# Merging the preparation into attention 0, and moving the split of the maxima ahead of the weight sums

## The reference

```python
mod = (_silu(L0_c) @ L0_wmod).reshape(16, 6, 1, -1)      # sa, ca, ga, sb, cb, gb; ga, gb kept at 0.25 or more in size
h = _layernorm(x) * (1 + ca) + sa
x = x + ga * attn0(h)        # 16 heads of 8; k and v through a 32-wide latent
h = _layernorm(x) * (1 + cb) + sb
x = x + gb * ffn0(h)         # ternary weights: 128 -> 512 -> 512 -> 512 -> 128, silu gate, two exact gelus
# block 1: the same frame with a second mod (L1), a causal attention of 4 heads with a memory, and 8 experts, top 2
```

## Time and profile before

| | |
|---|---|
| timed, three executions | 852.59, 853.60, 857.45 us |
| profiled execution | 857.48 us, span 855.7 us |
| mean granted TensorE clock | 0.939 |
| busy over the span | PE 85%, DVE 73%, ACT 63%, POOL 45% |
| preparation | 0.7 to 20.2 us |
| attention 0 | 21.1 to 321.2 us |
| ffn0, attention 1, router, experts | 322.2 us to the end |

### The profile page before, as it was taken

The page is one execution under the profiler, slowest core; times in us unless marked ns, Lnnn a source line. Parts: engine busy times, 40 slices in busy tenths (PEclk is TensorE's granted clock), DMA queues, the critical chain, the costliest instruction groups (busy, mean ns, idle before and its releaser), DMA issues. The chain is left out here.

```text
span 855.7 us, 17153 instructions
## 1 busy us (share of the span) xinstructions
PE 729.7 (85%) x5738; PEld 507.8 (59%) x5738; DVE 624.4 (73%) x1423; ACT 540.4 (63%) x1195; POOL 388.9 (45%) x484
## 2 busy tenths in 40 slices
PE   3367999999998886789999998489998939999996
PEld 3222333333333325788989998367776728888774
DVE  3176898998988525787777764278889857888884
ACT  0215777777776544668888885388887715655653
POOL 3533554645442001042111000489998625776664
PEclk9999999999999855999999999699999968999998
DMA  5365545444552004000000000000000250644430
GB/s 144 52 88 75 90 74 78 70 73 73 72 76 35 3 1 140 1 1 1 1 2 1 1 2 1 2 3 1 2 2 1 76 130 25 172 124 120 129 97 25
DMA packets 81178, 44.19 MB, mean 52 GB/s; under 512 B 7121, under 2 KB 79298, under 8 KB 80962
## 3 DMA queue, kind: packets, MB, share of 16 engines
q1 hardware_dynamic: 81090, 43.07, 25.3%
HBM read 27.83 MB, written 2.25 MB: 35 GB/s over the span
## 5 line engine op out<-in xcount | busy, mean ns | idle before, releaser
L597 DVE TENSOR_REDUCE att_negmax<-att_p_max 128x2 f32<-128x512 f32 x256 | 169.9, 687 | 42.4 <-PE att_p_max L481 40.1
L686 ACT ACTIVATE att_probs<-att_p_sT 128x1024 f32<-128x1024 f32 x128 | 130.9, 1025 | 60.2 <-PE att_p_sT L487 57.4
L481 PE MATMUL att_p_max<-att0p_QK 48*128 48x256 bf16 x512 | 102.8, 292 | 25.4 <-DVE att_negmax L597 11.6
L2061 POOL TENSOR_TENSOR moe_z_lo<-moe_z,moe_z_hi 128x512 fp32r<-128x512 f32 x64 | 96.8, 1525 | 55.1 <-ACT moe_z_hi L2014 54.5
L487 PE MATMUL att_p_sT<-att0p_QK 51*128 51x256 bf16 x512 | 101.5, 291 | 0.0
L952 POOL TENSOR_TENSOR ffn0s_rstd<-ffn0s_var_eps,top_minus_half 128x2 f32<-128x2 f32 x16 | 11.2, 700 | 191.9 <-DVE ffn0s_var_eps L939 191.9
L481 PEld LDWEIGHTS att_p_max<-att0p_QK 48*128 48x128 bf16 x512 | 29.1, 96 | 105.8 <-DVE att_negmax L597 50.2
L509 PE MATMUL att_p_o<-att_probs,att0p_V 128*32 128x256 f32 x1024 | 88.1, 419 | 0.1
L906 PE MATMUL ffn0s_p_h<-ffn0s_u_hi,top_ffn_all 128*128 128x256 f32 x256 | 71.3, 311 | 16.7 <-DVE ffn0s_u_lo L1167 16.2
L1167 DVE TENSOR_TENSOR ffn0s_g_lo<-ffn0s_g,ffn0s_g_hi 128x512 fp32r<-128x512 f32 x64 | 49.1, 782 | 43.8 <-ACT ffn0s_g_hi L1111 42.5
L2052 DVE TENSOR_TENSOR moe_z<-moe_act_u,top_ffn_all 128x512 f32<-128x512 f32 x64 | 73.1, 1143 | 2.2
(11 more groups left out here) (250 smaller groups left out, 1952.1 us busy)
## 6 DMA issues: line engine op xcount, KB each, us to landing
top_ffn_all<-combine SPq DMA_DIRECT2D x32, 512.0 KB, 6.6
att0p_QK<-att_parts SPq DMA_DIRECT2D x192, 64.0 KB
top_X<-in_L_attn_x SPq DMA_DIRECT2D x4, 512.0 KB, 7.0
att_raw<-in_L_ffn_h_w SPq DMA_DIRECT2D x8, 256.0 KB, 3.7
out_x<-top_X SPq DMA_DIRECT2D x8, 256.0 KB, 2.3
top_wo_all<-gates SPq DMA_DIRECT2D x4, 256.0 KB
top_gbo_all<-gates SPq DMA_DIRECT2D x4, 256.0 KB
top_wo_all<-gates SPq DMA_DIRECT2D x1, 1024.0 KB, 6.1
```

The costliest lines, as they stand in the source:

```text
L481: mm = pe.matmul(bank(at)[:, i, :], QK[r][rows, g, 0, i * P:(i + 1) * P], QK[r][rows, g, 1, :], start=True, stop=True)
L597: dve.tensor_reduce(negmax[:, :, w, g], bank(at)[:], AX.X, ALU.max, negate=True).then_inc(drained, 1)
L686: act.activation(probs[g % 2][:, t % 2], p_sT[t % 2][:], ACT.Exp).then_inc(exped, 1)
L2061: pool.tensor_tensor(z_lo[e % RING][:], z[e % RING][:], z_hi[e % RING][:].bitcast(F32), ALU.subtract).then_inc(z_lo_ready, 1)
```

## The change

1. `prepare` as a block is gone. `preparation(k, a, sb, sem, banks)` makes the same tensors inside `attention0` and hands out functions that the engines' programs call between their steps; its PSUM banks are those of the transposed scores.
2. The host packs the small inputs. `start_cols` [128 x 292] holds c of both blocks transposed, four bias columns, Wq and Wo with heads already in order; `start_rows` [32 x 385] holds Wl transposed, Wk, Wv and bl. x comes as [128 x 4096], so that a partition's share of several batches is one run in DRAM. PE's transposes of c and Wl and DVE's permutations go.
3. x is loaded in the parts `X_PARTS = [(0, 1), (1, 4), (4, 10), (10, 16)]` (batches), the first two at the start, the other two behind the stacks of batches 0 and 1. Each part and each modulation weight has its own semaphore.
4. Before step 0 only sa and ca of block 0 are made (4 of the 24 modulation instructions); the rest, the output bias and the gates come after step 1. The rows of the gates are stored in SP's step 1, and their loads move to steps 2 to 5, POOL's use of them to steps 3 to 6.
5. At the end the four sums stand in step 18 in slots 2, 6, 7 and 8, behind the split (slots 0 and 1). A product of a column of 0/1 marks with itself on PE counts the inexact rows in place of the way through DRAM, and the flag is made in step 19, slot 8.

```diff
+    def sp_loads(sp):
+        sp.dma_start(k.cols[:], a["start_cols"]).then_inc(c.cols_loaded, 16)
+        sp_x(sp, 0)
+        sp.dma_start(wmod[:, 0, :], a["L0_wmod"]).then_inc(wmod_loaded[0], 16)
+        sp.dma_start(rows[:], a["start_rows"]).then_inc(rows_loaded, 16)
+        sp_x(sp, 1)
+        sp.dma_start(wmod[:, 1, :], a["L1_wmod"]).then_inc(wmod_loaded[1], 16)
...
+    def pe_first(pe):
+        pe.wait_ge(rows_loaded, 16)
+        pe.matmul(p_v[:, 0:D], wlT, wk, start=True, stop=True)
+        pe.matmul(p_v[:, D:2 * D], wlT, wv, start=True, stop=True).then_inc(w_made, 1)
+        pe.matmul(p_b[:, 0:1], wk, lat_bias, start=True, stop=True)
+        pe.matmul(p_b[:, 1:2], wv, lat_bias, start=True, stop=True).then_inc(bias_made, 1)
+        pe.wait_ge(c_silu, 1)
+        pe.wait_ge(wmod_loaded[0], 16)
+        for j in (SA, CA):
+            mm = pe_mod(pe, 0, j)
+        mm.then_inc(mod_first_made, 1)
+        pe.wait_ge(c.ident_ready, 2)
...
+    def pe_rest(pe):
+        pe.wait_ge(c.bias_ready, 1)
+        pe.matmul(p_bo[:, 0:1], k.wo0, bv_col[:], start=True, stop=True).then_inc(bo_made, 1)
+        pe.wait_ge(c.mod_first_ready, 1)
+        for j in (GA, SB, CB, GB):
+            pe_mod(pe, 0, j)
+        pe.wait_ge(wmod_loaded[1], 16)
+        for j in range(6):
+            mm = pe_mod(pe, 1, j)
+        mm.then_inc(mod_rest_made, 1)
...
+                if n == B + 2 and slot in (2, 6, 7, 8):
+                    dve_sum_lo(dve, (2, 6, 7, 8).index(slot))
+                if n == B + 2 and slot == 9:
+                    dve_lo_any(dve)
+                    dve_lo_bad(dve)
+                if (n, slot) == FLAG_AT:
+                    dve_flag(dve)
...
-            if n == 0:
-                sp.wait_ge(gate_rows_ready, 1)
-                sp.dma_start(k.gates_dram, gate_rows[:]).then_inc(gates_stored, 16)
...
+            if n in (1, 2):
+                c.sp_x(sp, n + 1)
             if n == 1:
+                sp.wait_ge(gate_rows_ready, 1)
+                sp.dma_start(k.gates_dram, gate_rows[:]).then_inc(gates_stored, 16)
+            if n == 2:
                 sp.wait_ge(gates_stored, 16)
...
+        def pe_flag(pe):
+            at = RING["flag", 0]
+            pe.wait_ge(lo_bad_ready, 1)
+            at_least(pe, drained, at - 1)
+            pe.matmul(bank(at)[0:1, 0, 0:1], lo_bad[:], lo_bad[:], start=True, stop=True).then_inc(filled, 1)
...
+            c.pool_constants(pool)
+            c.pool_zero_v(pool, 0)
             pool_normalise(pool, 0)
+            c.pool_zero_v(pool, 1)
             for n in range(B + 3):
                 pool_step(pool, n, n % NB)
+                if n == 0:
+                    c.pool_zero_v(pool, 2)
+                    c.pool_zero_v(pool, 3)
...
-            pe_turn_gates(pe)
+            c.pe_first(pe)
             for n in range(LAST):
                 pe_step(pe, n, n % NB)
+                if n == 1:
+                    c.pe_rest(pe)
+                    pe_turn_gates(pe)
...
+            c.dve_ones(dve, 0)
+            c.dve_silu(dve)
             dve_stats(dve, 0)
+            c.dve_weights(dve)
+            c.dve_mod_first(dve)
+            c.dve_v_ones(dve, 0)
             for n in range(LAST):
                 dve_step(dve, n)
+                if n == 0:
+                    c.dve_ones(dve, 1)
+                    c.dve_v_ones(dve, 1)
+                if n == 1:
+                    for r in (2, 3):
+                        c.dve_v_ones(dve, r)
+                    c.dve_mod_rest(dve)
+                    for r in (2, 3):
+                        c.dve_ones(dve, r)
                 if n == B:
                     dve_scales(dve)
-                if n in (B + 1, B + 2):
-                    for quarter in range(2):
-                        dve_sum_lo(dve, 2 * (n - B - 1) + quarter)
-                if n == B + 2:
-                    dve_lo_any(dve)
-            dve_flag(dve)
```

More of the change, by code:

```diff
@@ L70 @@
 LATE_LOADED = 16 * LATE_LOADS
-X_LOADS = 4
-X_LOADED = 16 * X_LOADS
+X_PARTS = [(0, 1), (1, 4), (4, 10), (10, 16)]
+COLS = 2 * B + 4 + 2 * D
 class Names:
@@ L369, in attention0 @@
         p_m16 = p_m[:].bitcast(BF16)
+        c = preparation(k, a, sb, sem, [p_sT[n][:, w].rearrange("p i q -> p (i q)") for n in range(2) for w in range(2)])
         gates_turned = sem("gates_turned")
@@ L433, in attention0 @@
                     RING["O", n - 4] = len(RING)
+                if (n, slot) == FLAG_AT:
+                    RING["flag", 0] = len(RING)
                 if batch_valid(n - 2):
@@ L452, in pe_q @@
             pe.wait_ge(hT_ready, b + 1)
-            pe.matmul(p_m[:, 0:S], k.wq0[:], hT[:], start=True, stop=True)
+            if b == 0:
+                pe.wait_ge(c.wkv_ready, 1)
+            pe.matmul(p_m[:, 0:S], k.wq0, hT[:], start=True, stop=True)
         def pe_k(pe, b):
@@ L566, in pe_step @@
                     pe_turn_O(pe, t)
+                if (n, slot) == FLAG_AT:
+                    pe_flag(pe)
                 if slot >= SCORES:
@@ L837, in dve_scales, with dve_lo_bad @@
             dve.tensor_scalar(k.w3_gate[:], k.mod[:, 0, GB, :], k.w3_scale[:, 0:1], None, ALU.mult)
-        def dve_flag(dve):
-            dve.wait_ge(lo_row_loaded, 32)
-            dve.tensor_reduce(lo_flag[:, 0:1], lo_row[:], AX.X, ALU.max).then_inc(flag_step, 1)
-            dve.wait_ge(flag_step, 1)
-            dve.tensor_scalar(lo_flag[:, 1:2], lo_flag[:, 0:1], 0.0, None, ALU.not_equal).then_inc(flag_step, 1)
-            dve.wait_ge(flag_step, 2)
-            dve.tensor_copy(k.rows_inexact[:], lo_flag[:, 1:2])
+        def dve_lo_bad(dve):
+            dve.wait_ge(lo_any_ready, 1)
+            dve.tensor_scalar(lo_bad[:], lo_any[:], 0.0, None, ALU.not_equal).then_inc(lo_bad_ready, 1)
+        def pe_flag(pe):
[3 more added lines that the diff above has]
+            pe.matmul(bank(at)[0:1, 0, 0:1], lo_bad[:], lo_bad[:], start=True, stop=True).then_inc(filled, 1)
+        def dve_flag(dve):
+            at = RING["flag", 0]
+            dve.wait_ge(filled, at + 1)
+            dve.tensor_scalar(lo_flag[:], bank(at)[0:1, 0, 0:1], 0.0, None, ALU.not_equal).then_inc(drained, 1)
+            dve.wait_ge(drained, at + 1)
+            dve.tensor_copy(k.rows_inexact[:], lo_flag[:])
         def pool_step(pool, n, r):
@@ L2118, in build @@
         k.mod = sb("mod", [P, 2, 6, B])
-        k.wq0, k.wk0, k.wv0, k.wo0 = (sb(f"w{x}0", [P, D]) for x in "qkvo")
+        k.cols = sb("cols", [P, COLS])
+        k.wq0, k.wo0 = (k.cols[:, 2 * B + 4 + n * D:2 * B + 4 + (n + 1) * D] for n in range(2))
+        k.wk0, k.wv0 = (sb(f"w{x}0", [P, D]) for x in "kv")
         k.bq0, k.bk0, k.bo0 = (sb(f"b{x}0", [P, 1]) for x in "qko")
@@ L2137, in build @@
         k.mask16 = sb("mask16", [P, P], BF16)
-        k.flag_dram = nc.dram_tensor("flag", (P, 1), F32, kind="Internal").ap()
         k.bg = sb("bg", [P, E])
@@ L2196 @@
     arrays, aps = {}, {}
[L2197 to L2204 removed]
+    for name, array in laid_out(inputs).items():
         arrays[f"in_{name}"] = array
```

347 lines of the change are left out of this document (159 added, 188 removed).

## The result

The changed kernel took 846.6 us (median of 14 executions, 840.3 to 853.4) where the kernel before took 857.4 in the same rounds (851.2 to 864.9): a ratio of 0.9876, 95% interval 0.9842 to 0.9911. The profiled execution of the changed kernel took 841.4 us (span 839.5), 16.0 less than that of before.

The account below looks back on a forecast made before the run. Bounds: a latency chain at the start, TensorE at 1.2 GHz at the end. 857.5 less 12.5 (front), 1.8 (end) and 6.4 (clock) gave 836.8, or 832.9 from the median; forecast 835 us, range 829 to 846.

Parts of the forecast that it names:

- every later step has time to spare for its 262 KB: Gate loads, moved later: the last part costs the first weight load's step 0.3 us (0 to 1.9), later steps nothing.
- case A: End of attention 0: the clock drops all the same; 843.2 us, or 839.3 from the median; chance 0.36.
- First stack, 13.1 forecast: Start of the kernel: the first stack is issued at 13.1 us instead of 29.56, a gain of 16.5.
- Rival C: Start: loads don't land by need, TensorE starts at 9.93; front gains 7.9, time 847.8 or 843.9 us; chance 0.12.
- Second stack at 28.4, held by the gate rows: SP's queue: stack 1 waits for the gate rows' store and goes out at 28.4 for 43.68; 15.2 us left.
- Memsets to 30.4: VectorE, before batch 0's first maximum: two memsets of 1.76 us hold it until 30.4; 13.9 us of gain left.
- The front's sum of 12.5: Start through the first stacks: total gain of 12.5 us, between 9.1 and 15.2.
- the 1.1 and 0.3 taken for bytes: Loads behind the stacks: surplus bytes behind stack 1 cost 1.1 us, the gates' last part 0.3.
- The end, 8.2: End of attention 0: 1.8 us from the reordered split, sums and flag, and 6.4 from the clock staying up.
- Case B: End of attention 0: without idle time for the split the clock stays up, 6.4 us; the forecast, chance 0.48.
- Rival D: Steady stretch: the clock swing strikes there; at 45 us of lower clock 21 us lost, time 864; chance 0.04.
- The sign that the prediction had named against itself: Steady stretch: more than 209 us for the same steps would show the prediction wrong.

Follow-up runs that it names:

- the last experiment: Changed kernel with all addresses as before modulo 512, and x of batches 4 to 9 and 10 to 15 loaded one step later; one execution took 838.6 us.

## Why the prediction was wrong

**The step that failed** is the one that gave the steady stretch nothing: "as every later step has time to spare for its 262 KB", and with it a sum in which 209 us of unchanged instructions keep their length. They had no time to spare. In the old trace each stack is issued as the one before lands (stack 1 at 43.68, stack 2 at 58.73), in the first steps and, at 14.93 us apiece, in nearly all later ones. The engines need 14.91 for a step, as the runs with quick addresses show, so the chain of transfers was level with TensorE (busy 195 of 209 us). Anything that lengthens a stack then goes into the time in full, and the change did: it moved the stacks' target by 160 bytes, which nothing in the prediction weighed, and a stack took 0.7 us more. With the addresses put back the same change takes 835.6 us, where 835 had been forecast. The steady stretch was 7.1 us longer than before; with the addresses put back it is 8.9 shorter (226.3 for 235.2), and the medians lie 11 us apart.

**The accounts.** The sum on the profiled execution was 836.8. Plus 7.1 for the steady stretch, less 1.8 by which the end did better, is 842.1; it took 841.4, and the later stages were 1.0 shorter. The change's median lies 5.2 above its profiled execution, where before's lies on it. The profiled one was among the quickest of 14, whose mean granted clock ran from 0.939 to 0.957. The longest had the lowest, so the clock may have a part in it; where, only profiled executions could show. The range was to hold case A with the front's worst, and by the prediction's own numbers that is 843.2 + 3.4 = 846.6, not 846.

**First stack, 13.1 forecast:** 13.75; the rows landed 0.8 later than taken (5.3 + 1.8 + 0.9 is 8.0; the prediction went on with 8.1). Rival C is out: TensorE began at 6.06, not at 9.93.

**Second stack at 28.4, held by the gate rows:** their store went out at 28.00, but stack 1 at 30.03, when stack 0 had landed: 16.3 us after its issue for 14.1. One microsecond of that was the x behind it (the last experiment), another the address (15.3 with the old ones). The prediction priced x on the stacks behind it and not on the one in front. It read the Trainium skill's ring order (DMA: Bandwidth & Descriptors, "Queues, rings and completion order") as x costing the stack in front nothing; the trace disagrees, with 15.3 us for 14.3. What x cost the stacks behind it no run separates.

**Memsets to 30.4:** to 30.86, and the first maximum at 30.79. Stack 0 landed at 30.03 and the first score tile began at 30.06, and without memsets in the way the first maximum began 0.6 after that tile (27.67 after 27.03, the run without them). So they cost about 0.1 here; where stack 0 landed early they cost 2.7. **The front's sum of 12.5** was right by errors that cancel: the 1.1 and 0.3 taken for bytes were really stack 1, issued 1.6 late behind stack 0 and 16.2 us under way for the 15.1 taken, so that it and not the memsets' step opened the next. With the old addresses 14.0 came out (first maxima of the second batch, 45.51 for 59.47), within 9.1 to 15.2.

**The end, 8.2:** 10.0. No wait of TensorE for the split is left (284.46 follows its work without idle time), the four sums start in VectorE's gaps, and its last operation is a residual sum. From the split's transposes to the last product with V TensorE took 16.8 us, where 17.9 had been walked. Case B held in the profiled execution, and the sums put back show the cause, though not a certain one. Rival A and the Trainium skill's rule behind it (TensorE: Matmul & The Clock Gate, "A second HAM failure mode: psum-queue depth-cycling") fit the steady stretch better: the fall to 0.52 at 186 us came after an idle time of TensorE amid steady work. The rule speaks of short idle times, and this one was 2.0 us.

**Rival D** had the place right and the mechanism half: the steady stretch did lose, but mostly to longer stacks. The low clock struck one step and, with the wait ahead of it, cost 3.5 of the 7.1 us. The sign that the prediction had named against itself, a steady stretch longer than before for the same steps, is the one that came (235.2 us for 228.2 from the second batch's first maximum to the last).

**Left open:** why the target's address matters this way (256 best, 32, 96 and 128 worst), why the change's median lies 5.2 us above its profiled execution, and why the sums cost 13 us or more between timed runs at the slow addresses and 8 at the quick ones.

## What to carry to other kernels

Read a diff also for the tiles whose size it changes: everything allocated behind them moves, and a transfer like these (SBUF to SBUF, rows of 512 bytes) whose target moves off a multiple of 256 bytes took 9 to 30% longer alone on the chip, without a line of its code being touched. Put the targets of such transfers, where they set the pace, at multiples of 256; a pad of 160 bytes was worth 10 to 14 us here, as much as the whole change. And before a stretch is written down as unchanged, look for what it waits at once per step: where each transfer is issued as the last one lands, there is no slack to hide anything in.

## What the runs showed of the hardware that was not expected

- SBUF to SBUF, 512-byte rows: a stack of 786 KB alone on the chip took 12.3 to 12.6 us with the target at a multiple of 256 (11.2 and 11.4 once each), 13.6 to 14.3 at 64 or 192 past one, and 14.6 to 16.2 at 32, 96, 128 or 224 past; the source's address made no difference. Two of its twelve DMAs move rows of 1,024 bytes.
- In the kernels the same shows in the mean time of a 512-byte packet over the stacks of batches 5 to 14: 36 to 39 ns with the target at a multiple of 256, 53 to 55 with the old address, 62 with the changed one, and 65 and 64 with 32 bytes more in the changed kernel and in the old.
- Small transfers issued among a stack's took 2.2 us to their last recorded landing with the target at a multiple of 256, 3.2 to 3.7 with the old address, and 4.2 to 4.3 with the others.
- 32 unused bytes per partition made the kernel before 1.2% slower.
- The same 1.59 us of idle time of TensorE was followed by the lower clock in four profiled executions and not in a fifth.
